# Graph kernel: edge fields unpacked in fp16 with rounding keys, and out-degrees counted ahead of the last products

## What is computed

```python
h = relu(layernorm(x))
deg = segment_sum(1, src)                       # out-degrees
feat = h * clip(deg, 1)**-0.5
x = x + relu(segment_sum(feat[src], dst)) @ W.T + b           # layer 0
h = relu(layernorm(x))
msg = h[src] @ W_msg.T + b_msg + edge_embed[edge_type]
m = segment_sum(msg, dst)
x = x + gru_cell(m, h)                                         # layer 1
```

## Time and profile before

| | |
|---|---|
| median of three runs | 977.11 us (976.65 to 979.45) |
| profiled execution, its own time | 977.03 us |
| its span, first to last instruction | 975.24 us |
| busy, PE | 848.3 us (87%) |
| busy, DVE | 805.4 us (83%) |
| busy, ACT | 516.9 us (53%) |
| busy, POOL | 70.5 us (7%) |
| mean granted clock of TensorE | 0.984 |

### The profile page before, as it was taken

One profiled execution on the slowest core, in us unless ns is written; L12 is line 12 of the kernel. 1 busy time (PEld: TensorE's weight loads), 2 busy tenths in 40 slices (PEclk: granted clock), 3 DMA queues, 4 the chain that ended last, 5 costly groups with the idle time before them and its releaser, 6 DMA issues.

```text
span 975.2 us, 21134 instructions
## 1 busy us (share of the span) xinstructions
PE 848.3 (87%) x8908; PEld 754.0 (77%) x8908; DVE 805.4 (83%) x1177; ACT 516.9 (53%) x1055; POOL 70.5 (7%) x71
## 2 busy tenths in 40 slices
PE   1244689999999999999999999899999999999993
PEld 1133578888888888888888888788898888988882
DVE  4989999999999999999999993186677666776666
ACT  5786267888888888787888886111111111111110
POOL 5670100101001010000000000000000000000000
PEclk9999889999999999999999999999999999999997
DMA  6432304634335543344433330557766677666740
GB/s 140 111 98 108 143 20 184 238 146 163 138 143 224 200 162 146 143 162 200 184 147 139 143 138 12 128 196 275 274 241 242 249 277 282 235 247 245 274 164 12
DMA packets 38739, 169.99 MB, mean 174 GB/s; under 512 B 8156, under 2 KB 21667, under 8 KB 35696
## 3 DMA queue, kind: packets, MB, share of 16 engines
q1 hardware_dynamic: 32332, 160.84, 43.6%
q0 software_dynamic: 6000, 6.48, 2.7%
q10 hardware_dynamic: 308, 1.28, 0.5%
HBM read 88.52 MB, written 80.00 MB: 173 GB/s over the span
## 4 chain that ended last, share of the span: by engine, by line
PE 46%; DVE 41%; ACT 7%; DMA 3%; issue 2%; SPq 0%; DVEq 0%
PE ps L1209 25%; DVE work L692 14%; DVE work L699 11%; PE ps L1087 8%; PE ps L1076 4%; DVE work L705 4%; ACT ring L880 3%; PE ps L1175 2%; PE ps L1176 2%; ACT junk L892 1%; DMA tab<-dst 1%; PE ps L1180 1%; PE ps L1179 1%; ACT junk L953 1%; DVE pst L716 1%
## 5 line engine op out<-in xcount | busy, mean ns | idle before, releaser
L1076 PE MATMUL ps<-work 128*128 128x106 f16 x3125 | 430.6, 216 | 69.4 <-ACT ring L880 57.9
L1087 PE MATMUL ps<-ring,tab 125*128 125x250 f16 x2500 | 418.7, 274 | 3.1 <-DVE tab L677 2.5
L880 ACT ACTIVATE ring<-ps 128x848 f16<-128x848 f32 x375 | 329.6, 882 | 89.1 <-PE ps L1076 83.2
L1076 PEld LDWEIGHTS ps<-work 128*128 128x128 f16 x3125 | 288.1, 101 | 91.4 <-ACT ring L880 59.2
L1209 PE MATMUL ps<-ring,tab 125*128 125x250 f16 (+1 forms) x2500 | 276.8, 269 | 0.0
L1087 PEld LDWEIGHTS ps<-ring,tab 125*128 125x128 f16 x2500 | 245.5, 99 | 28.9 <-DVE tab L677 2.7
L1209 PEld LDWEIGHTS ps<-ring,tab 125*128 125x128 f16 (+1 forms) x2500 | 242.4, 97 | 28.6
L692 DVE TENSOR_TENSOR work<-iota_lo,mch 128x3150 f16<-128x3150 f16 x125 | 226.3, 1810 | 9.9 <-ACT mch_s L864 4.9
L699 DVE TENSOR_TENSOR work<-iota_w,mch 128x1250 f16<-128x1250 f16 x250 | 193.9, 818 | 0.0
L777 DVE TENSOR_TENSOR work<-work,ring 125x3250 f16<-125x3250 f16 (+1 forms) x92 | 161.8, 1780 | 0.0
L1031 ACT ACTIVATE raw<-ps,bg 128x250 f32<-128x250 f32 x50 | 20.7, 467 | 176.1 <-PE ps L1176 176.1
(11 more groups left out here) (156 smaller groups left out, 607.6 us busy)
## 6 DMA issues: line engine op xcount, KB each, us to landing
adjacency<-ring SPq DMA_DIRECT2D x23, 2937.5 KB
ring<-adjacency SPq DMA_DIRECT2D x46, 812.5 KB, 6.3
ring<-adjacency SPq DMA_DIRECT2D x46, 750.0 KB, 9.1
adjacency<-ring SPq DMA_DIRECT2D x23, 183.1 KB
h_turned<-hst SPq DMA_DIRECT2D x25, 125.0 KB, 2.0
raw<-h_turned SPq DMA_DIRECT2D x25, 125.0 KB, 2.1
out<-x_sb SPq DMA_DIRECT2D x25, 125.0 KB
x_sb<-x SPq DMA_DIRECT2D x3, 560.0 KB
```

Of the source, the lines that this page charges most:

```text
L880: act.activation(to(x * 2 * u, 2, x), ps[:, s:s + 2, 0:x * SLOTS].rearrange("p b (x h) -> p h b x", h=SLOTS), ACT.Copy).then_inc(sem("evac ...
L1076: last = pe.matmul(ps[:, 2 * (u % 2) + i // BANKW, o:o + WCOLS], lohot[:, s, k, :], combo[:, s, k, :], start=True, stop=True)
L1087: mm = pe.matmul(psD[c % 2], tabv[0][P, h, s, :], adj[c % 2][P, h, :], start=i == 0, stop=i == 2 * BLOCKS - 1)
```

## The change

Unpacking. The row is no longer rounded with MAGIC in fp32. KEY = 1025 is added to it and the result is written as fp16: between 1024 and 2048 fp16 holds whole numbers alone. All keys carry the 1025: `f_lo`, `f_ta` and the place `t_c`; the iotas that they are compared with carry it too (`iota_row` replaces `iota_lo` in L692, `iota_t[:, 0]` begins at 1025, `thr_key` = `thr` - 1025), and it cancels in the differences. `iota_w` now steps by 50 from one destination block to the next. Three of the four temporary tiles are fp16, and one is fp32. Ten instructions in four steps; the wait on `turned` moves from the second step to the first.

Counting. From chunk 20 of layer 1 on, VectorE makes five additions per chunk instead of four, each one part further ahead, so that in m = 23 the last four of the 100 parts are (24, 0) to (24, 3), where before (24, 0) and (24, 1) stood at the end of m = 23 and the two others in m = 24. The folds and the comparison are mixed with the gate, state and output of chunk 23 and stand before the gate of chunk 24; the state of chunk 24 comes before the wait for the flag's sum.

```diff
-        temps = sb("temps", [128, 4, AHEAD * EDGES_MAX], F32)
+        temps = sb("temps", [128, AHEAD * EDGES_MAX], F32)
+        temps_h = sb("temps_h", [128, 4, AHEAD * EDGES_MAX], F16)
...
+            gp.iota(thr_key[:, :], [[WIN, CHUNKS]], base=-KEY, channel_multiplier=BLOCKS,
+                    allow_small_or_imprecise_dtypes=True)
+            gp.iota(iota_row[:, :], [[1, LO + 1]], base=KEY, channel_multiplier=0, allow_small_or_imprecise_dtypes=True)
...
-            ch.did(v.tensor_scalar(t_q, e_src, 1.0 / BLOCKS, 0.5 / BLOCKS - 0.5, ALU.mult, ALU.add))
-            ch.did(v.tensor_tensor(t_d, e_dst, spread(thr[P, g:g + n], [LO, n, EDGES_MAX]), ALU.subtract))
+            positive(v, sem("turned"), g + n - FRING)
+
+            ch.did(v.tensor_scalar(f_lo, e_src, 1.0 / BLOCKS, KEY + 0.5 / BLOCKS - 0.5, ALU.mult, ALU.add))
             ch.did(v.tensor_scalar(t_t, e_typ, 0.0, float(TYPES - 1), ALU.max, ALU.min))
+            ch.did(v.tensor_tensor(t_d, e_dst, spread(thr_key[P, g:g + n], [LO, n, EDGES_MAX]), ALU.subtract))
             done = ch.k
             yield
             ch.wait_to(done)
-            positive(v, sem("turned"), g + n - FRING)
-            ch.did(v.tensor_scalar(f_lo, t_q, MAGIC, MAGIC, ALU.add, ALU.subtract))
-            ch.did(v.tensor_scalar(t_d, t_d, -1.0, float(WIN), ALU.max, ALU.min))
-            ch.did(v.tensor_scalar(t_a, t_t, float(TB), None, ALU.is_ge))
+            ch.did(v.tensor_scalar(f_ta, t_t, 1.0 / TB, KEY - 1.0 / TB, ALU.mult, ALU.add))
+            ch.did(v.tensor_scalar(t_c, t_d, KEY - 1.0, float(KEY + WIN), ALU.max, ALU.min))
             done = ch.k
             yield
             ch.wait_to(done)
-            ch.did(v.scalar_tensor_tensor(t_q, f_lo, -float(BLOCKS), e_src, ALU.mult, ALU.add))
-            ch.did(v.scalar_tensor_tensor(f_ta, t_t, float(2 * TB), t_a, ALU.is_ge, ALU.add))
...
+            ch.did(v.tensor_tensor(t_n, t_c, f_lo, ALU.subtract))
+            ch.did(v.tensor_tensor(t_k, t_c, f_ta, ALU.subtract))
...
-            ch.did(v.scalar_tensor_tensor(f_col, t_d, float(SLOTS), t_q, ALU.mult, ALU.add))
-            ch.did(v.scalar_tensor_tensor(t_t, f_ta, -float(TB), t_t, ALU.mult, ALU.add))
-            done = ch.k
-            yield
-            ch.wait_to(done)
-            v.scalar_tensor_tensor(f_small, t_d, float(TB), t_t, ALU.mult, ALU.add).then_inc(sem("fields"), n)
+            ch.did(v.scalar_tensor_tensor(f_col, t_n, float(BLOCKS), e_src, ALU.mult, ALU.add))
+            v.scalar_tensor_tensor(f_small, t_k, float(TB), t_t, ALU.mult, ALU.add).then_inc(sem("fields"), n)
             yield
...
+            for m in range(1, last):
+
+                to = 4 * (m + 1) + max(0, m + 5 - last)
+                parts = [divmod(i, 4) for i in range(counted, to)]
+                counted = to
+                add_counts(v, *parts[0])
+                add_counts(v, *parts[1])
                 post1_gate_vector(v, ch, m - 1)
-                add_counts(v, m, 2)
+                add_counts(v, *parts[2])
                 post1_state_vector(v, ch, m - 1)
-                add_counts(v, m, 3)
+                add_counts(v, *parts[3])
                 post1_out_vector(v, m - 1)
...
+                for part in parts[4:]:
+                    add_counts(v, *part)
             v.wait_ge(sem("added"), 4 * CHUNKS)
...
+            fold_counts(v, ch, 124, 126)
+            fold_counts(v, ch, 62, 64)
+            post1_gate_vector(v, ch, last - 1)
+            fold_counts(v, ch, 32, 32)
+            post1_state_vector(v, ch, last - 1)
+            compare_degrees(v, ch)
+            post1_out_vector(v, last - 1)
             post1_gate_vector(v, ch, last)
+            post1_state_vector(v, ch, last)
             v.wait_ge(sem("flag_sum"), 1)
             v.tensor_scalar(flag_i[:, :], psFlag, 0.0, None, ALU.is_gt).then_inc(sem("flag_set"), 1)
-            post1_state_vector(v, ch, last)
             post1_out_vector(v, last)
```

## The result

| | before | after |
|---|---|---|
| median | 976.88 us (4 runs, 975.86 to 979.45) | 965.57 us (4 runs, 963.37 to 966.52) |
| profiled execution, its own time | 977.03 us | 966.52 us |
| its span | 975.24 us | 964.5 us |
| busy, PE / DVE / ACT | 848.3 / 805.4 / 516.9 us | 849.2 / 797.8 / 516.5 us |
| mean granted clock of TensorE | 0.984 | 0.986 |

The ratio of the times is 0.9878, with a 95% interval from 0.9858 to 0.9897: 11.3 us less, where 14.25 was forecast. The time lies inside the range, 2.8 us above the predicted 962.8. Lines have moved: L692 is L698 now, L699 is L705, L705 is L711, L726 is L732, L777 is L783, L788 is L794, L1076 is L1094; the ten unpacking instructions are L552 to L571.

What follows compares the result with a forecast made beforehand. VectorE was taken to bound the build at 62.36 us per triplet, TensorE just below at 60.03. Six triplets 6.2, start 1.2 and 0.5, tail 6.35: 14.25 off 977.03 gives 962.8 us, range 959.6 to 966.6.

Steps and rivals of the forecast that it cites:

- Step 5: Unpacking of three chunks in the build: instruction L565 goes, 0.38 us less per triplet.
- step 3: Unpacking in the build: L553 and L554 become two fp16 subtractions, 0.48 us less per triplet.
- Rival 1: The build gives half, from a floor near 61.9 per triplet or fp16 subtractions gaining nothing: 966.4 us, chance 0.10.
- step 4: Unpacking in the build: L560 and L561 become `f_col` and `f_small`, 0.05 us more per triplet.
- step 1: Unpacking in the build: L540 goes and `f_lo` comes, written to three rows with gaps, 0.22 us more per triplet.
- step 2: Unpacking in the build: `t_c` and `f_ta` replace L547, L548 and L549, 0.44 us less per triplet.
- The start: Unpacking before the build's loop: 1.2 us less for chunks 3 to 5, 0.5 less for chunk 0.
- The tail: End of layer 1: the last gate follows ACT's sigmoids instead of the folds and comparison, 6.35 us less.
- rival 3: End of layer 1: chunk 24's first quarter lands late and blocks a gate; 964.8 us if at 938.3, chance 0.05.
- Rival 2: Only the end of layer 1 gains; VectorE's waits at batch 2 eat the build's saving: 970.7 us, chance 0.03.
- Rival 4: Slower: constants and `temps` move in SBUF, slowing L692 and L699 in the build; 987 us at 8%, chance 0.02.
- Rival 5: VectorE cuts off when writing fp16, keys are wrong and the general path runs: thousands of us, chance 0.01.

Runs made afterwards that it cites:

- norm_b3: The changed kernel with the norm made behind batch 3 instead of batch 4 and ACT's square root one unit earlier: 953.14 us, ratio 0.9756 to the kernel before.

## Why the prediction was right or wrong

**The floor under the triplet: wrong, and the reason why the build gave 2.0 of 6.2.** The step that failed is the reading of 20.01 as TensorE's own pace, and with it "That lands at 61.3 per triplet, well above 60.03, so VectorE still sets the pace and the gain is whole". The 20.01 is the loop's pace: 16.17 from batch 0 to batch 4 and 3.84 to the next batch 0. What the triplet needed was the same sum by chunk. Timeline of VectorE, batches 0 and 4 of two chunks (the middle one and the one behind it), before and then after:

```profile
241.87 1.80 DVE L692 TENSOR_TENSOR work<-iota_lo,mch 128x3150 f16<-128x3150 f16 x1
...
259.31 1.79 DVE L692 TENSOR_TENSOR work<-iota_lo,mch 128x3150 f16<-128x3150 f16 x1
...
263.14 1.80 DVE L692 TENSOR_TENSOR work<-iota_lo,mch 128x3150 f16<-128x3150 f16 x1
...
279.32 1.91 DVE L692 TENSOR_TENSOR work<-iota_lo,mch 128x3150 f16<-128x3150 f16 x1
```

```profile
238.31 1.80 DVE L698 TENSOR_TENSOR work<-iota_row,mch 128x3150 f16<-128x3150 f16 x1
...
255.50 1.79 DVE L698 TENSOR_TENSOR work<-iota_row,mch 128x3150 f16<-128x3150 f16 x1
...
259.33 1.80 DVE L698 TENSOR_TENSOR work<-iota_row,mch 128x3150 f16<-128x3150 f16 x1
...
275.48 1.80 DVE L698 TENSOR_TENSOR work<-iota_row,mch 128x3150 f16<-128x3150 f16 x1
```

From batch 0 to batch 4 three chunks in a row took 16.21, 17.44 and 16.18 before: two of the three stood on the loop's 16.15 already. Only the middle one had anything to give, and it gave 0.25 (17.44 to 17.19). Step 5's 0.38 and step 3's 0.48 fell in the other two and turned into waits. The chain of before does hold both steps, as VectorE was the last to arrive there, but by 0.06 us at most: a place on that chain says that work counts, not how much of it can be saved. Rival 1 named this floor, with the same waits (norm, ACT, banks), and priced it rightly (61.9 and 966.4; measured 61.98 and 965.57), but it shared a chance of 0.10 with another cause, slow fp16 subtractions, which fell. What was held against it, the 60.40 of the triplet with one chunk, does not speak against it: of the 1.96 by which that stretch is shorter, 1.28 is the middle chunk's (17.44 to 16.16) and 0.63 step 4's (4.84 to 4.21 from batch 4 to the next batch 0), which stands ahead of the norm in the loop. The rest of the 0.38 is in stretches that gave under 0.1 each. Triplets at 62, the prediction's own first sign of being wrong, are what came. The error could have been seen before the run: the wait of ACT (L920) for VectorE's norm (L726) is used in the prediction's first part to put step 4 on the chain, and was not followed once round.

**Prices: right.** From start to start of the batches around them, step 1 costs 0.24 more (forecast 0.22), step 2 0.47 less (0.44), step 3 0.45 less (0.48), step 5 0.47 less (0.38), all four nearly the same with the loop in place and with it cut. Step 4 costs 0.06 more with the loop cut (forecast 0.05 more; 0.03 less with the loop). The five come to 1.09 less with the loop cut, for a forecast of 1.03, and the triplet gave 1.11. These are lengths by form in after (busy us, mean ns):

```profile
L570 DVE SCALAR_TENSOR_TENSOR fields<-temps_h,raw 125x384 f16<-125x384 f16 x7 | 5.0, 720 | 0.0
L552 DVE TENSOR_SCALAR fields<-raw 125x384 f16<-125x384 int32 x7 | 4.9, 706 | 0.0
L571 DVE SCALAR_TENSOR_TENSOR fields<-temps_h 125x384 f16<-125x384 f16 x7 | 3.9, 558 | 0.0
L563 DVE TENSOR_TENSOR temps_h<-temps_h,fields 125x384 f16<-125x384 f16 x7 | 3.2, 451 | 0.0
L553 DVE TENSOR_SCALAR temps_h<-raw 125x384 f16<-125x384 int32 x7 | 3.1, 449 | 0.0
L558 DVE TENSOR_SCALAR fields<-temps_h 125x384 f16<-125x384 f16 x7 | 3.1, 449 | 0.0
L564 DVE TENSOR_TENSOR temps_h<-temps_h,fields 125x384 f16<-125x384 f16 x7 | 2.4, 345 | 0.0
```

`f_small` (L571) is all fp16 and takes 558 ns, as long as L561 with its fp32 operand (549). `f_ta` (L558), fp16 into three rows, takes 449, where L547 from fp32 took 649. `f_lo` (L552) and `t_t` (L553) read the same tile of integers with the same step, and the one that writes three rows takes 706, the other 449. Each agrees with what the prediction drew from the Trainium skill ("Vector Engine (DVE) Microarchitecture Reference", section 5.1).

**The start: right.** Chunks 3 to 5 gave 1.3 for a forecast of 1.2, chunk 0 0.6 for 0.5.

**The tail: right.** The last gate fell from 9.79 us behind ACT's message to 3.44, 6.35 as forecast. Gate 22 waits 1.95 where it waited 4.21; in the chunks before it 2.58 is left (forecast 2.4). The first quarter of chunk 24, issued at 923.2, is waited for (0.41), and its addition ends 1.95 before the gate: that wait on a DMA ahead of a gate is one of the prediction's signs of being wrong, and the load that rival 3 named is the one, but it held back no gate. The two folds end at 944.61 and the gate of chunk 23 starts at 945.46; with the 4.4 us that after is ahead there, that is 949.0 and 949.9, for 948.9 and "near 950".

**The other rivals and theory C** fell. Rival 2: the triplet did shrink, by 0.38, and unpacking at the start by 1.9. Rival 4 and C: L698 takes 1800 ns, as L692 did in the earlier trace rows, and `norm_b3` recovers the loss with the same transfers and the same placement. Rival 5: no general path ran.

**What hides the rest.** The loop gave 2.0 for 6.2, so 4.2 us are missing. Against it stand 1.2 more at the start; 0.5 was lost before the tail (a transfer at the start of layer 1, `tab` from `dst`, took 14.07 us for 13.56), 0.3 gained in it beyond the forecast and 0.4 lost behind it: 14.25 - 4.2 + 1.2 - 0.5 + 0.3 - 0.4 = 10.65, for a measured 10.7. So the time came within 2.8 us of the forecast although the triplets gave a third of their 6.2: the tail came as forecast, and 1.0 of the start is luck, as the kernel was quicker there ahead of the unpacking. And the profiled execution is the longest of its four, 0.95 above their median. These smaller terms are of the size by which the start of the build differs between runs (112.5 to 113.7 in the kernels with the new unpacking); no run tested them, and their causes stay open.

## What to carry to other kernels

A stretch that repeats itself exactly, without the work in dispute, is not yet one engine's own pace: follow the chain once round, and ask whether the engine that you make quicker feeds what it waits for. Then add up its work piece by piece between two such waits, not over the whole period, for a saving counts only in a piece that is longer than the loop. Where a loop is found, moving the link that closes it (here one call, a batch earlier) can be worth more than the work that was to be saved: 12.4 us against 4.9.

## What the runs showed of the hardware

A memset of 384 fp32 elements on 128 partitions shows as 0.38 us in the timeline; a triplet grew by 0.34 where VectorE bounds the chunk, by 0.39 with the loop cut, and not at all in the chunk that the loop held. Two instructions of one form side by side, L563 and L564, show 451 and 345 ns, but 0.18 and 0.26 on the chain: in `norm_b3` L563 starts at 263.04, 0.28 before the record of L711 ahead of it ends, so a pair is to be priced together (0.44).
